# Last expert stage: the place of the row weighting behind the copies, and where the last turn's exponentials are summed

## The reference

```
router_probs = softmax(x_flat @ gate_w)
expert_idx   = argmax(router_probs)
expert_w     = router_probs[expert_idx]
out[row]     = expert_w * (gelu(x @ w1[e] + b1[e]) @ w2[e] + b2[e])     # e = expert_idx of the row
x            = x + out
```

## Time and profile before

| | us |
|---|---|
| median of 3 runs | 1688.08 (1687.92 to 1692.17) |
| the profiled execution, its own time | 1681.99 |
| span of the profiled execution | 1680.2 |
| TensorE busy (share of the span) | 1406.2 (84%) |
| VectorE busy | 1117.5 (67%) |
| ScalarE busy | 893.0 (53%) |
| GpSimd busy | 771.6 (46%) |

### The profile page before, as it was taken

One profiled execution on the slowest core, in us unless ns is written; L12 is line 12 of the kernel. 1 busy time (PEld: TensorE's weight loads), 2 busy tenths in 40 slices (PEclk: granted clock), 3 DMA queues, 4 the chain that ended last, 5 costly groups with the idle time before them and its releaser, 6 DMA issues. The chain is left out here.

```text
span 1680.2 us, 37485 instructions
## 1 busy us (share of the span) xinstructions
PE 1406.2 (84%) x10866; PEld 1302.5 (78%) x10867; DVE 1117.5 (67%) x3513; ACT 893.0 (53%) x2687; POOL 771.6 (46%) x766
## 2 busy tenths in 40 slices
PE   6768699937777489999999999999997599566498
PEld 4656599935566389999999999999996599354387
DVE  5656544458867367778787877777776466686355
ACT  4455155522322178787777777878773133233254
POOL 4067244420004354556657565757463366104344
PEclk9797799977767699999999999999998699777599
DMA  9312122240321300000000000000000333701322
GB/s 219 45 37 61 43 62 65 63 171 1 105 71 32 119 14 2 14 1 19 9 18 8 17 8 16 9 0 13 1 14 14 114 83 85 233 8 59 110 84 61
DMA packets 88412, 88.54 MB, mean 53 GB/s; under 512 B 17058, under 2 KB 74761, under 8 KB 87927
## 3 DMA queue, kind: packets, MB, share of 16 engines
q1 hardware_dynamic: 72472, 58.10, 12.7%
q0 software_dynamic: 12448, 26.21, 4.7%
q10 hardware_dynamic: 3392, 3.02, 0.7%
HBM read 53.98 MB, written 34.82 MB: 53 GB/s over the span
## 5 line engine op out<-in xcount | busy, mean ns | idle before, releaser
L2150 POOL TENSOR_TENSOR paired_rows<-paired_rows,rinv 128x1024 f32<-128x1024 f32 x128 | 242.6, 1895 | 243.7 <-DVE rinv L2465 227.3
L2456 DVE TENSOR_TENSOR probs_turned_lo<-psum_banks,probs_turned_hi 128x512 fp32r<-128x512 f32 x256 | 175.8, 687 | 141.5 <-ACT probs_turned_hi L2315 137.9
L2341 ACT ACTIVATE paired_rows<-psum_banks,neg_max 128x256 f32<-128x256 f32 x512 | 237.2, 485 | 0.6 <-DVEq L2042 0.4
L2262 PE MATMUL psum_banks<-probs_turned_hi,y_rows 128*128 128x256 f32 x1024 | 214.0, 292 | 0.9 <-DVEq L2042 0.9
L2212 PE MATMUL psum_banks<-y_turned_parts,queries_hi 128*128 128x256 f32 x1024 | 199.9, 293 | 3.0 <-DVEq L2042 3.0
L2262 PEld LDWEIGHTS psum_banks<-probs_turned_hi,y_rows 128*128 128x128 f32 x1024 | 167.3, 190 | 1.7 <-DVEq L2042 1.5
L2315 ACT CAST probs_turned_hi<-psum_banks 128x512 fp32r<-128x512 f32 x256 | 151.3, 591 | 19.3 <-PE psum_banks L2183 9.4
L2212 PEld LDWEIGHTS psum_banks<-y_turned_parts,queries_hi 128*128 128x128 f32 x1024 | 158.3, 191 | 3.6 <-issue 3.6
L2183 PE MATMUL psum_banks<-ident,paired_rows 128*128 128x128 f32 x1024 | 155.6, 274 | 5.3 <-DVE probs_turned_lo L2456 2.9
L2471 DVE TENSOR_REDUCE neg_max<-psum_banks 128x4 f32<-128x1024 f32 x128 | 155.5, 1215 | 5.0 <-PE psum_banks L2212 4.7
L2212 PE MATMUL psum_banks<-y_turned_parts,queries_lo 128*128 128x256 f32 x512 | 145.0, 283 | 0.0
(11 more groups left out here) (716 smaller groups left out, 3736.6 us busy)
## 6 DMA issues: line engine op xcount, KB each, us to landing
paired_rows<-expert_rows SPq DMA_DIRECT2D x16, 512.0 KB, 6.0
expert_w_a<-rows_by_expert_last SPq DMA_DIRECT2D x39, 129.0 KB
tile_rows<-rows_by_expert_first SPq DMA_DIRECT2D x71, 64.5 KB
tile_rows<-rows_by_expert SPq DMA_DIRECT2D x71, 64.5 KB
expert_w_b<-in_L_ffn_w_dram SPq DMA_DIRECT2D x2, 2048.0 KB, 13.1
tile_rows<-expert_rows SPq DMA_DIRECT2D x8, 512.0 KB, 3.8
x_rows<-in_x_dram SPq DMA_DIRECT2D x8, 256.0 KB, 5.4
ctx_turned_dram<-ctx_turned SPq DMA_DIRECT2D x1, 2048.0 KB, 10.4
```

The lines of the kernel that those rows point to most:

```text
L2150: ins = pool.tensor_tensor(probs[:, k, :, :], probs[:, k, :, :], rinv[:, k, :].unsqueeze(2).to_broadcast([P, 4, 256]), ALU.mult)
L2262: ins = pe.matmul(bank[Z_BANK][:, r * 256:(r + 1) * 256], yrows[:, 2 * s1 + y, (2 * r + k) * P:(2 * r + k + 1) * P], probsT[x][:, (u + 1) ...
L2341: ins = act.activation(probs[:, par, h, :], bank[S_BANKS[par] + h // 2][:, (h % 2) * 256:(h % 2 + 1) * 256], ACT.Exp, bias=nmax[:, par, h: ...
L2456: ins = dve.tensor_tensor(lo, bank[bank_][:, :], hi.bitcast(F32), ALU.subtract)
```

## The change

In the last expert stage the drain between sum and weighting goes. The sum signals a counter of its own, `banks_read`, for which TensorE's L1578 now waits in place of `expert_kept`. The weighting moves behind the two copies of the same step; it waits on `banks_read` for its own tile's sum, and signals `expert_kept` as before.

In the last turn of attention a stream's exponential becomes four ScalarE instructions of 128x8, each of which also sums its eight numbers into `exp_sum`; VectorE's reduction and its drain go. The first turn, whose 16 groups are done together, keeps one exponential and the reduction.

The rest of the diff takes out branches for layers that don't scatter their rows (all four do, `SCATTERED = (0, 1, 2, 3)`) with eleven semaphores and the functions of an older gather; none of that was run.

```
...
+        banks_read = counter("banks_read")
...
     def rows_out(j, u):                          # TensorE
...
                             if beyond(j, 2):
-                                pe.wait_ge(expert_kept.sem, j + (expert_kept.value - 1))
+                                if layer == 3:
+                                    pe.wait_ge(banks_read.sem, j + (banks_read.value - 1))
+                                else:
+                                    pe.wait_ge(expert_kept.sem, j + (expert_kept.value - 1))
...
     def step(k, u):                              # VectorE
...
                             slot_is_free(dve, j, s)
-                            ins = dve.tensor_tensor(yo[:, s, :], bank[6 + s % 2][:, 0:P], b2[:, bass.ds(off, P)], ALU.add)
-                            if layer == 3:
-                                dve.drain()
-                                ins = dve.scalar_tensor_tensor(yo[:, s, :], yo[:, s, :], xr[:, s, LAST_WEIGHT:LAST_WEIGHT + 1], xr[:, s, P:2 * P], ALU.mult, ALU.add)
-                            ins.then_inc(expert_kept.sem, 1)
+                            dve.tensor_tensor(yo[:, s, :], bank[6 + s % 2][:, 0:P], b2[:, bass.ds(off, P)], ALU.add).then_inc((banks_read if layer == 3 else expert_kept).sem, 1)
                         j, s = k + 2, (u + 2) % SLOTS
                         if exists(j):
...
                             if not fixed:
                                 dve.tensor_copy(w1[:, s % 4, :], W1[:, bass.ds(off, WIDE)]).then_inc(weights_placed.sem, 1)
+                        j, s = k - 1, (u - 1) % SLOTS
+                        if layer == 3 and exists(j):
+                            dve.wait_ge(banks_read.sem, j + (banks_read.value + 1))
+                            dve.scalar_tensor_tensor(yo[:, s, :], yo[:, s, :], xr[:, s, LAST_WEIGHT:LAST_WEIGHT + 1], xr[:, s, P:2 * P], ALU.mult, ALU.add).then_inc(expert_kept.sem, 1)
...
     def exp_of(own, n):                          # ScalarE, attention_3
                         act.wait_ge(last_leads.sem, n)
-                        act.activation(expo[:, own, :], expo[:, own, :], ACT.Exp).then_inc(last_leads_exp.sem, 1)
+                        if own.stop - own.start == N:
+                            ins = act.activation(expo[:, own, :], expo[:, own, :], ACT.Exp)
+                        else:
+                            for n_ in range(own.start, own.stop):
+                                ins = act.activation(expo[:, n_, :], expo[:, n_, :], ACT.Exp, accum_out=exp_sum[:, n_:n_ + 1])
+                        ins.then_inc(last_leads_exp.sem, 1)
...
     def row_weights(i, own, n):                  # VectorE, attention_3
                         dve.wait_ge(last_leads_exp.sem, n)
-                        ch.link(dve.tensor_reduce(exp_sum[:, own], expo[:, own, :], AX.X, ALU.add))
+                        if own.stop - own.start == N:
+                            ch.link(dve.tensor_reduce(exp_sum[:, own], expo[:, own, :], AX.X, ALU.add))
                         return dve.reciprocal(LAST_ROWS[:, i * N + own.start:i * N + own.stop, LAST_WEIGHT], exp_sum[:, own])
```

More of the change, by code:

```diff
@@ L222, in build @@
         pairs_summed = counter("pairs_summed")
-        gathered = [counter("gathered_even"), counter("gathered_odd")]
-        rows_here = counter("rows_here")
         pairs_here = [counter(f"pairs_here{w}") for w in range(W)]
@@ L227, in build @@
         tile_loaded = [counter(f"tile_loaded{i}") for i in range(SLOTS)]
-        tile_stored = [counter(f"tile_stored{i}") for i in range(SLOTS)]
         tile_scattered = [counter(f"tile_scattered{i}") for i in range(SLOTS)]
@@ L549, in combine_stream @@
         def combine_stream(dve, ch, i, w, layer):
[L551 to L554, removed]
+            dve.wait_ge(pairs_here[w].sem, i * 16 + (pairs_here[w].value + 16))
             combine(dve, ch, i * W + w, layer)
@@ L571, in combine @@
                     xt = flat(X[:, bass.ds(t, 1), :])
-                    row = YY[:, bass.ds(t, 1), k, :] if layer in SCATTERED and slots == 2 else (XN, Y1)[k][:, bass.ds(t, 1), :]
+                    row = YY[:, bass.ds(t, 1), k, :]
                     ins = dve.scalar_tensor_tensor(xt, flat(row), WT[:, k, bass.ds(t, 1)], xt, ALU.mult, ALU.add)
@@ L1430, in experts @@
             LAG = 6
-            scatters = layer in SCATTERED
             kept = layer in KEPT
             arrived = tile_loaded if layer in KEPT else sorted_in
-            expert_out = tile_scattered if scatters else tile_stored
+            expert_out = tile_scattered
             with ExitStack() as ph:
@@ L1511, in _ @@
                             sp.wait_ge(ctx_back.sem, 16)
[L1513 to L1523, removed]
                 @block.gpsimd
@@ L1532, in _ @@
                         i = j - LAG
-                        if scatters and i >= 0:
+                        if i >= 0:
                             pool.wait_ge(expert_kept.sem, i + (expert_kept.value + 1))
@@ L1540, in _ @@
                             pool.indirect_dma_start(ys, bass.IndirectOffsetOnAxis(ap=to, axis=0), yo[:, i % SLOTS, :], None).then_inc(expert_out[i % SLOTS].sem, 16)
-                    if scatters:
-                        for s in range(SLOTS):
-                            pool.wait_ge(expert_out[s].sem, expert_out[s].value + 16 * in_slot(s))
+                    for s in range(SLOTS):
+                        pool.wait_ge(expert_out[s].sem, expert_out[s].value + 16 * in_slot(s))
                 @block.tensor
@@ L1719, in close_rows @@
         def close_rows(layer):
-            if layer in SCATTERED:
-                for c in pairs_here:
-                    c.value += 16 * TURNS
-            else:
-                close_gathers(CHOICES[layer])
+            for c in pairs_here:
+                c.value += 16 * TURNS
         def load_expert_weights(sp, layer):
@@ L1742, in load_expert_weights @@
             done.value += 16 * len(srcs)
-        def gather_turns(pool, layer):
-            top = CHOICES[layer]
-            for g in range(NG + 1):
-                if g < NG:
-                    gather_group(pool, g, top)
-                if g >= 1:
-                    group_is_here(pool, g - 1, top)
         def attention_1(layer_before):
```

16 lines of the change are left out of this document (removed).

## The result

In the first measurement, four runs of each kernel, the changed kernel took 1673.01 us (median, 1671.42 to 1677.99) and the kernel before 1688.0 us (1686.52 to 1692.17); ratio 0.9912, 95% interval 0.9885 to 0.994. Two repeats on other occasions gave 1677.36 us and 0.9947 [0.9927, 0.9966] in 11 runs, and 1677.18 us and 0.9952 [0.993, 0.9974] in 9 runs. It is faster: in the larger measurements by 8 to 9 us going by the ratios on record (the medians themselves lie 10.8 and 9.2 us apart), in the smallest by 15 us.

What follows compares the result with a forecast made beforehand. VectorE's sequencer, held by the drain, was taken to bound the last expert stage. 7.0 us there plus 0.5 in attention made 7.5 us off the 1688.08 us median: 1680.6 us, range 1678.3 to 1687.4.

Steps and rivals of the forecast that it cites:

- the loop body: Last expert stage, eight tiles: from 18.38 to 16.7 us, bounds 16.2 and 17.4; four bodies gain 6.8 us.
- attention: Last turn of attention: summing exponentials gain 0.55 us, bounds -0.3 and 0.75, of which 0.5 us arrives.
- the half clock: First expert-stage tiles run at half clock until 1590.3; if that moment stays, only 0.3 of attention's 0.55 us arrives.
- the loop's edge: Last expert stage: TensorE's extra per body at the loop's edge, 0.35 us, estimated from VectorE's 0.67 on the first edge round.
- the saving is a matter of instructions in a fixed place: Whole kernel: the 7.5 us off the profiled execution also comes off the runs' median of 1688.08, giving 1680.6 us.
- The price of the wait and the sending: Last expert stage, VectorE: added semaphore wait and moved sending of the weighting cost 0.15 us a tile, between 0.12 and 0.20.
- the tiles behind the loop: Last expert stage: tiles ahead of and behind the loop together gain 0.2 us.
- the 0.2 us that I subtracted: Attention, stream 1: second-half roots queue behind the exponential on ScalarE, 0.6 us to spare against 0.8 delay, losing 0.2 us.
- TensorE keeps 2.14 us a tile: Rival, last expert stage: TensorE does not take up the slack, only edges get cheaper; gain 1 to 5 us, chance 0.20.
- the sum still holds the sequencer: Rival, last expert stage: register reads can't start while the sum runs; stage unchanged, gain 0.5, 1687.6 us, chance 0.07.
- The ring: Rival, last expert stage: eight slots close as later weighting delays scatter and reload; slower, 1693 us, chance 0.04.
- the "issue" wait: Sign, last expert stage: VectorE's wait on its own sequencer ahead of the row copy gets about 0.36 us shorter per tile.

Runs made afterwards that it cites:

- drain kept: Changed kernel, weighting still behind the copies, but with a drain behind the sum again; 1693.73 us in one run, body 18.96 us.
- clean-up alone: Kernel before with only the never-run branches and eleven semaphores taken out; 1686.71 us, ratio to the kernel before 1.0001 [0.9983, 1.002].
- the exponentials: Kernel before with the never-run code taken out and the four summing exponentials, expert stage as before; 1685.02 us, ratio 0.9996 [0.9978, 1.0013].
- the move: Changed kernel with one exponential and VectorE's reduction back in the last turn of attention; 1679.32 us, ratio to the kernel before 0.9955 [0.9933, 0.9977].
- between copies: Changed kernel with the weighting between the row copy and the weight copy; 1681.43 us in one run, body 16.99 us.
- no weighting: Changed kernel with the weighting's arithmetic left out, a bare semaphore increment behind the same wait; 1673.52 us in one run, body 16.70 us.
- the wait in place: Changed kernel with the weighting back right behind the sum, held by a wait on banks_read instead of the drain; 1685.28 us in one run.

## Why the prediction was right and where it was wrong

I had forecast 1680.6 us, 7.5 us less, in a range down to 1678.3. The first measurement, 1673.01 us, lies outside, 15 us less. The mechanism held: the move frees the sequencer and the loop body falls to what was forecast. What failed is the range, and by smaller amounts the size of three terms, attention, the half clock and the loop's edge.

**What failed first is the range**, at the step "the saving is a matter of instructions in a fixed place, so it comes off there too". I subtracted from the median of three runs and gave the range only the bounds of the costs, nothing for the medians themselves. The repeats' medians lie at 1677.2 and 1677.4 us, below the range as well, and those of the kernel before moved from 1686.4 to 1688.9 between measurements. Put as a ratio, the forecast was 0.9956 and the lower end of the range 0.9942: the forecast lies inside both larger intervals and outside the first, and both larger ratios, 0.9947 and 0.9952, lie in the range. So of the first 15 us some 6 are not the change's but those of a median of four runs; this rests on the two repeats. (The low bound of the body, 16.2 us, was a slip besides: VectorE alone, at 0.25 us less a tile, would need 16.4.)

**The loop body: right.** 16.7 us forecast, 16.86, 16.80 and 16.69 measured. The row copy starts 0.36 us sooner behind the sum, the weighting 1.36 us behind it where I had said 1.4, TensorE took up the slack. The price of the wait and the sending, 0.15 us a tile in my sum, can't be read here, for TensorE is the limit; with the drain kept, most rounds grew by 0.07 us or less. In the body from 1620.68 its five plain tiles take 1.89 to 2.11 us, mean 2.02 as taken, but three tiles at the loop's edge take 2.20, 2.28 and 2.27: 0.69 us extra where I gave the edge 0.35, an estimate from VectorE's rounds that no row of TensorE stood behind. Four bodies brought 4 x (18.36 - 16.78) = 6.3 us against 6.8 forecast, the tiles behind the loop 0.5 against 0.2.

**Attention: 0.88 us instead of 0.5 in the traces.** The two traces are 4.79 us apart at the first turn's scatters, ahead of the edits (1536.47 and 1531.68), and 3.91 at stream 2's: stream 0 brought 0.28, streams 1 and 2 0.60. The exponentials took 0.88 us for four instead of 1.0, and behind stream 1's they are followed at once by the roots (1556.31), which VectorE uses at 1556.98, right behind its reciprocal at 1556.89: the 0.2 us that I subtracted were not lost. The cast-to-reciprocal distance fell from 0.33 to 0.08 us, the 0.25 forecast. The other traces repeat the first stretch in nine of twelve and the second in all twelve. In timed runs the edit by itself shows 0.04% with an interval of 0.17% to either side, which neither shows nor excludes 0.9 us.

**The half clock.** I had discounted the attention gain for it. From the first to the fourth tile's first product it took 7.56 us before and 6.27, 6.58 and 6.13 us after, but 7.11 with the clean-up alone, 6.40 with the exponentials and 7.69 with the move. It varies by 1.5 us with the moment at which the granted clock rises from 0.50 to 1.00. Counted from stream 2's first scatter that moment comes at 25.0 to 25.9 us in nine traces and at 26.5 to 28.1 in six. The three without the exponentials are all among the late ones (27.6, 26.5, 27.7), but so are three with them: drain kept, between copies and no weighting (27.9 to 28.1, and 7.5 to 7.7 us from the first to the fourth product). So neither edit decides it by itself; that the exponentials make the early moment likelier is possible and not shown. It gave the traces of the changed kernel 1.0 to 1.4 us beside the one of before, where my sum had given the half clock nothing but a small loss.

**The sum by traces.** 0.88 for attention and 109.6 - 101.8 = 7.8 or, with the other two traces, 8.2 to 8.3 us for what follows: 8.7 to 9.2 us, against 8.1 and 8.9 from the two larger ratios. Without what the half clock gave, it is 7.4 to 8.2 us, around the 7.5 forecast; that the forecast came so near is in part luck, since the body gained 0.5 us less than I had summed and attention and the tiles behind the loop 0.7 more.

**The rivals.** That TensorE keeps 2.14 us a tile fell with the body. That the sum still holds the sequencer, the rival of the Trainium skill's page "VectorE: DVE Perf Modes", section "The DRAIN you can't avoid", fell with the 0.82 us between sum and row copy. By that section a later VectorE instruction starts only when the pipe is empty, unless it is one that isn't held, which starts earlier. The trace shows the second: the weight copy starts at 1601.03 and the row copy ahead of it, from 1600.83, lasts 0.29 us. Register reads go on beside a running instruction: the one at 1620.00 begins 0.15 us into a row copy of 0.29 us. The trap was next to it: the wait in place shows that a wait for the sum's end stops the sequencer. The ring did not close, with about 2 us to spare.

**One of the signs that I had named was wrong.** I had said that the "issue" wait ahead of the row copy would shrink by 0.36 us a tile. It is 17.3 us in 32 tiles, 0.54 each, where it was 0.49. The idle time before an instruction is counted from the end of the one before it, and the weighting, whose 0.35 us had filled a part of the gap, has left it. The distance from sum to row copy is the quantity to watch, and it fell.

## What to carry to other kernels

An engine with register reads between its instructions can be bound by its sequencer before it is bound by its arithmetic: look in the chain for what holds the sequencer, as the drain did here for 0.36 us a tile, and put an instruction that depends on its predecessor behind others that don't, since a wait in the same place freed next to nothing (0.05 us). When that is done, read who waits for whom again: here the engine that had waited became the bound at once, and leaving out the whole weighting brings only 0.2 us a body. Compare distances between two fixed points of the trace rather than spans, and don't put a narrow range on a median of three runs.

## What was not expected of the hardware

- A wait for the engine's own last instruction cost 0.32 us from start to start where the drain cost 0.36.
- A 128x516 copy on VectorE takes 0.42 us, and up to 0.71 us when it starts 0.52 to 0.79 us into GpSimd's indirect transfer, all such copies ending 1.22 to 1.26 us behind the transfer's start, but still 0.42 when it starts sooner in it; the transfer takes 0.97 us alone and mostly 1.15 to 1.16 when it starts second.
- A memset of 0.55 us with a drain ahead of an indirect transfer cost GpSimd 2.06 us a round (3.04 us from one transfer to the next, 0.98 of it the transfer).
- With TensorE's first products 4.4 us sooner, the granted clock still rose from 0.50 to 1.00 at 25.3 and 25.9 us behind stream 2's first scatter, against 25.1 to 25.2.
- Summing exponentials of 128x8 follow each other every 0.20 us, those of 128x128 every 0.35 us.
